# Shared expert of an MoE layer on one core: routing slots before the first chunk, and the row scatter's schedule

## The reference

```
logits = xf @ gate_w.T                      # 8 columns
probs  = softmax(logits); top 2, weights divided by their sum
shared = (silu(xf @ sw_gate) * (xf @ sw_up)) @ sw_down      # widths 256, 352, 256
shared = sigmoid(xf @ shared_gate_w.T) * shared
expert = the same gated form with w_gate[e], w_up[e], w_down[e]
x      = x + shared + sum over the token's 2 experts of weight * expert(xf)
```

## Time and profile before

| | us |
|---|---|
| median of 3 runs | 3038.25 |
| lowest and highest of them | 3037.5, 3042.67 |
| the profiled execution | 3054.86 |
| its span, first to last instruction | 3052.9 |
| stage `l1s` in it, from 980 to the first instruction of `l1e` | 980.1 to 1148.1 |

### The profile page before, as it was taken

One profiled execution on the slowest core, in us unless ns is written; L12 is line 12 of the kernel. 1 busy time (PEld: TensorE's weight loads), 2 busy tenths in 40 slices (PEclk: granted clock), 3 DMA queues, 4 the chain that ended last, 5 costly groups with the idle time before them and its releaser, 6 DMA issues. The chain is left out here.

```text
span 3052.9 us, 55088 instructions
## 1 busy us (share of the span) xinstructions
PE 2470.2 (81%) x20060; PEld 1589.0 (52%) x20060; DVE 2077.8 (68%) x5408; ACT 1273.6 (42%) x2332; POOL 1029.7 (34%) x1438
## 2 busy tenths in 40 slices
PE   1998368999617678996979887995899999969973
PEld 0444354666415347995546543444565555646662
DVE  5997746666467655665577787877766545866667
ACT  1887333333113212332347655871322222257722
POOL 3551470100254341113557478961300000025330
PEclk9998688999857889998989897996899999979996
DMA  4661555333321237775644134420200000024301
GB/s 117 178 183 52 175 210 140 96 83 107 111 79 44 76 110 264 259 259 174 222 115 100 41 104 106 92 40 3 66 22 1 1 1 1 1 53 103 74 10 61
DMA packets 320320, 300.08 MB, mean 98 GB/s; under 512 B 193244, under 2 KB 268298, under 8 KB 314037
## 3 DMA queue, kind: packets, MB, share of 16 engines
q1 hardware_dynamic: 293364, 220.28, 25.7%
q0 software_dynamic: 17904, 76.23, 7.3%
q10 hardware_dynamic: 8784, 0.04, 0.2%
HBM read 166.60 MB, written 88.34 MB: 84 GB/s over the span
## 5 line engine op out<-in xcount | busy, mean ns | idle before, releaser
L1717 ACT ACTIVATE l2e_hf<-l2e_H 128x512 f32<-128x512 f32 x208 | 124.2, 597 | 383.6 <-PE l2e_H L1658 383.6
L1871 POOL TENSOR_TENSOR all_m_rstd<-all_m_sq,all_mhalf 128x8 f32<-128x8 f32 x24 | 39.6, 1649 | 561.9 <-DVE all_m_sq L1856 527.0
L1658 PE MATMUL l0e_H<-l0e_xT,l0e_w 128*128 128x512 f16 x768 | 169.9, 383 | 27.7 <-DVE l0e_w L1736 27.7
L1771 DVE CAST l2e_hh<-l2e_hf 128x512 f16<-128x512 f32 x208 | 92.7, 446 | 123.5 <-ACT l2e_hf L1717 109.3
L805 DVE TENSOR_REDUCE l0a_mx<-l0a_S 128x2 f16<-128x512 f32 x256 | 162.3, 680 | 11.1 <-PE l0a_S L653 10.9
L1658 PE MATMUL l2e_H<-l2o_hi,l2e_w 128*128 128x512 f16 x576 | 152.5, 383 | 15.8 <-DVE l2e_w L1736 15.8
L801 DVE CUSTOM_DVE_ANT_0 l2s_masked<-l2s_S,l2s_mq 128x128 f32<-128x128 f32 (+1 forms) x512 | 149.4, 346 | 21.7 <-PE l2s_S L653 19.7
L1717 ACT ACTIVATE l0e_hf<-l0e_H 128x512 f32<-128x512 f32 x128 | 76.4, 597 | 207.4 <-PE l0e_H L1658 207.4
L1658 PE MATMUL l1e_H<-l1e_xT,l1e_w 128*128 128x256 f16 (+1 forms) x1404 | 158.7, 275 | 4.3 <-DMA l1e_w<-packed,all_second_weight_row 4.3
L761 ACT ACTIVATE l0a_pf<-l0a_ST 128x512 f32<-128x512 f32 x256 | 147.1, 610 | 23.3 <-PE l0a_ST L667 23.1
L1658 PE MATMUL l2e_H<-l2e_hh,l2e_w 128*128 128x512 f16 x640 | 155.1, 379 | 0.0
(11 more groups left out here) (687 smaller groups left out, 6999.0 us busy)
## 6 DMA issues: line engine op xcount, KB each, us to landing
l0e_wf<-in_L_ffn_w SPq DMA_DIRECT2D x16, 1024.0 KB, 7.3
rows<-l0a_zeros SPq DMA_DIRECT2D x16, 640.0 KB, 6.0
l1e_rb<-rows SPq DMA_DIRECT2D x39, 256.0 KB, 9.7
results<-l1e_y SPq DMA_DIRECT2D x39, 256.0 KB, 2.2
l0a_kv<-in_ctx SPq DMA_DIRECT2D x16, 512.0 KB, 4.2
rows<-l0a_zeros SPq DMA_DIRECT2D x16, 512.0 KB, 5.0
l0d_p_cx<-in_ctx SPq DMA_DIRECT2D x16, 512.0 KB, 5.9
results<-l0e_y SPq DMA_DIRECT2D x16, 512.0 KB, 3.0
```

Of the source, the lines that this page charges most:

```text
L1658: mm = pe.matmul(bank[0:fn, :], W[par][0:kn, at + k * wd + f0:at + k * wd + f0 + fn], X, start=(done == 0), stop=(done == k_all - 1))
L1717: nc.scalar.activation(hf[q % 4][0:fn, :], pair_of(q, lay)[0][0:fn, :], lay.func, scale=1.0 / WS).then_inc(acted, 1)
L1771: nc.vector.tensor_copy(high, v).then_inc(hi_done, 1)
L1871: self.nc.gpsimd.tensor_tensor(out=(self.rstd, self.rstd2)[which][:, g], in0=(self.sq, self.sq2)[which][:, g], in1=self.g.mhalf[:, 0:self. ...
```

## The change

It does four things, all in stage `l1s`:

- `rank` on PE and `copy_ranks` on ACT stand in front of the third chunk (q = 2), where they stood in front of the second unit (q = 3).
- DVE runs all of `assign` in one go, after `choose` and before its work on the first chunk.
- ACT makes the high halves of parts 0 to 3 first of all, ahead of the conversion of the shared weights; DVE makes the low halves of parts 0 and 1 there, and those of parts 2 and 3 right after `assign`.
- The calls are renumbered: with `BEHIND` = 0 and `EVERY` = 7, calls 0 to 3 are the four made ahead, and parts 4 to 7 fall on calls 10, 17, 24 and 31. Call 4 is the first chunk's, so part 4 goes with the first down tile of round 1, part 5 with the last, part 6 with the first down tile of round 2 and part 7 with the last.

```diff
@@ tensor queue
                 for un in plan:
-                    if router is not None and un is plan[1]:
-                        router.rank(pe)
...
                             q = un.at + f
                             before = bank_free[q]
+                            if router is not None and q == 2:
+                                router.rank(pe)
                             if before is not None:
@@ scalar queue
                 copy(0)
+                for _ in range(send.ring if send is not None else 0):
+                    send.hi_part(nc, act)
                 for k in of_expert[0]:
                     convert(k)
...
                 for un in plan:
-                    if router is not None and un is plan[1]:
-                        router.copy_ranks(act)
...
                             q = un.at + f
+                            if router is not None and q == 2:
+                                router.copy_ranks(act)
@@ vector queue
                     router.split(dve)
+                for _ in range(2 if send is not None else 0):
+                    send.lo_part(nc, dve)
                 for k in of_expert[0]:
                     convert(k)
...
                 assigning = router.assign(dve) if router is not None else iter(())
+                for _ in assigning if send is not None else ():
+                    pass
+                for _ in range(send.ring - 2 if send is not None else 0):
+                    send.lo_part(nc, dve)
@@ class Send
-    GQ, BEHIND, EVERY = 4, 11, 6
+    GQ, BEHIND, EVERY = 4, 0, 7
```

## The result

The change made the kernel slower: 3050.53 us (median of 6 runs, 3045.13 to 3051.33) against 3038.12 of the kernel before beside it (6 runs, 3036.9 to 3042.67), a ratio of 1.003 with a 95% interval of 1.002 to 1.004. The forecast was 3031. The profiled execution took 3051.33 (span 3049.6), 1 us more than its median.

The account below looks back on a forecast made before the run. Without lag, POOL's scatter bounds stage `l1s` before (1117) and PE's chain after (1106.2 + 3.7 = 1109.9), a gain of 7 us: 3038.25 - 7 = 3031. Range 3021 to 3046.

Parts of the forecast that it names:

- the first case: Stage `l1s`: no lag in timed runs, POOL bounds the kernel before; 3031 us (3028 to 3034), chance 0.45.
- the gain of 7 us: Stage `l1s` without lag: its end moves from POOL's 1117 to PE's 1110.
- the lag: Stage `l1s` during the scatter: PE halts and its finished work reaches others late; second-round down tiles lose 38.3 us.
- the second case: Stage `l1s`: lag at full size in timed runs, PE bounds both kernels; -1 to +4 us, 3037 to 3042, chance 0.32.
- I had 3.7: PE in `l1s`: late start at chunk 2 leaves it 3.7 us later after two rounds.
- the 3.6 us at the end may go: End of `l1s`: DVE's last packing began 3.6 us late; with the scatter over by then, this may vanish.
- one burst only: POOL's scatter in `l1s`, lag at full size: a burst of again 40 DMAs, keeping 38.3 us of PE's loss.
- The third case: Stage `l1s`: lag becomes longer, POOL issuing 48 DMAs in one go instead of 40; 3048 to 3052, chance 0.12.
- chunk 2 taken up 17 us later: PE in `l1s`: waits for DVE's slots and low halves, taking up chunk 2 at 1014.4, 16.6 us later.
- PE's chain alone: PE in `l1s`, kernel before without lag: its own work would end the stage at 1106.2.
- POOL's end: POOL's scatter in `l1s`, kernel before without lag: done at 1114.8, with landing and change of stage 1117.
- The ring: ACT in `l1s`: part 5's high half waits for part 1 to be sent; nothing lost, up to 1 us.

Follow-up runs that it names:

- batch D: The second batch with the lag in which both unaltered kernels ran: changed kernel 3052.18 us, kernel before 3046.65 us (29 runs).
- e10: Kernel before, with only the halves of parts 0 to 3 made ahead, all four low halves too: 0.9992 of the kernel before.
- e5: Changed kernel, unaltered, run again in a batch without the lag: 2992.61 us, 0.9947 of the kernel before.
- e16: Changed kernel with three memsets on POOL before each part but the first, in a batch with the lag: 3023.73 us, 0.9927 of the kernel before.
- e3: Changed kernel with ten memsets on POOL before each part but the first, in a batch without the lag: 1.0081 of the kernel before.
- e4: Changed kernel with one memset on POOL after each scatter DMA, in a batch without the lag: 1.0145 of the kernel before.
- e7: Changed kernel with three memsets on POOL before each part but the first, in a batch without the lag: 1.0001 of the kernel before.
- e8: Changed kernel with a very small memset (128x16) on POOL after each DMA, in a batch without the lag: 1.007 of the kernel before.
- e6: Kernel before, unaltered, run again in a batch without the lag: 0.9994 against itself.
- e15: Kernel before, with each of the four packings' low halves made twice on DVE, in a batch with the lag: 1.0021 of the kernel before.
- e12: Kernel before, with three memsets on POOL before each part but the first, in a batch without the lag: 1.004 of the kernel before, +14.2 us.

## Why the prediction was wrong

**The step that failed** is the choice of the first case, 0.45 for "no lag in the timed runs", and with it POOL as the bound of the kernel before, which alone gave the gain of 7 us. It rested on two things. One was the 16.6 us between the profiled execution of the kernel before and its median. The other was what the Trainium skill ("NOTIFIC — the notification-queue block", section "7.1 Overflow: three behaviours, one of which stalls the engine") says of the block that writes the records, that it holds its producers back rather than lose one. I took the lag for the work of a recording that timed runs don't have.

The lag was in the timed runs. With it, the profiled time of the changed kernel lies within 2 us of its median in both batches (3051.33 against 3050.53, 3050.31 against 3052.18), and breaks in the scatter bring 22 us in the median. The 16.6 us were no measure of it: that execution was already 9.5 us behind the changed kernel's at the start of the stage (980.11 against 970.63), where both kernels are still the same, and in batch D, which has the lag, 29 runs of the kernel before spread over 17 us (3036.8 to 3053.9). An unexplained difference between one execution and a median told how much the time varies, not that the lag was absent.

Whether the recording has a part in the lag is not settled by this. Every run here, not only the profiled one, comes with a span and a granted clock, so none is known to be free of records; and the traces with lag are the ones in which landing times are missing.

**What the runs showed in its place** is the second case, the lag at full size. I gave it 0.32 and -1 to +4 us, and its mechanism held: PE bound in both, lag 38.3 us in both, series of 40 DMAs in both. Its size was off: +5.3 us in the stage. After two rounds the changed kernel is 3.5 us behind in the stage (1087.17 - 970.63 against 1093.16 - 980.11); I had 3.7. Then "the 3.6 us at the end may go": the last tiles take 4.8 us less (8.1 instead of 12.9) and the two rounds of chunks 0.9 less, but 6.2 came in the third round's tiles. Parts 6 and 7 were sent in one series of 16 DMAs (24.4 us), as they had been before (1111.36 to 1134.2), and now this series ends in a round of down tiles with work left behind it. I had counted one burst only. With 1.3 us more at the change of stage the sum is 3.5 - 4.8 - 0.9 + 6.2 + 1.3 = 5.3 us, 168.0 to 173.4. The second batch's timed difference agrees (5.5). The first batch's 12.4 is 7 more, and no trace shows where; the spread of the kernel before in batch D is larger than that, in the first batch (5.8) it isn't. The third case, a longer first lag, did not come: part 5 was handed over only after it, as worked out. That its 3048 to 3052 holds the measured 3050.5 is luck.

**Right:** the first DMA 19.3 to 20.0 us earlier (20 predicted), chunk 2 taken up 17 us later (16.6), no wait at chunk 8 with the lag, 4.0 us for PE without the scatter (3.7), and a stage of 125.5 us for PE's chain alone (126.1, from 980.1 to 1106.2). The early high halves cost nothing to be seen (e10, 0.9992).

**Mis-sized, in the first case's sum.** Where there is no lag the gain was 14.3 us of stage (15.8 timed), not 7.

- *POOL's end, 13.7 us too early.* I had 137.0; it was 150.7. The DMAs from the first to the end of the last took 89.6 us, not 82.8, because packings and low halves on DVE hold POOL up: 6.8. I had named this rule and given it "about 1 us". From the end of the last DMA to the next stage it took 7.5, not 2.2: 5.3. And POOL started 1.6 later in this trace. Two of the three stood in the first trace, in stage `l0d`: its last DMA starts 8.1 us before the next stage's first load, and its slow DMAs lie beside packings.

```profile
437.14 2.42 DVE L2995 SCALAR_TENSOR_TENSOR l0d_pk_wp<-l0d_pk_wf,l0d_pk_wp 128x2176 f16<-128x2176 f32 x1
...
437.32 3.08 POOL L2622 DMA_INDIRECT rows<-l0d_parts,all_first_write  x1 [0.30 <-issue]
...
453.47 0.97 POOL L2622 DMA_INDIRECT rows<-l0d_parts,all_first_write  x1 [0.30 <-issue]
461.56 1.90 SPq L1519 DMA_TRANSPOSE l0e_xT<-rows  x1
```

- *The ring, 6.6 us instead of 0 to 1.* Without a lag POOL is behind PE, and ACT stands for part 1 to be sent before it may make part 5's high half (row of ACT in e5); chunks 6 to 11 take 22.2 us instead of the 15.5 of the later rounds. PE's chain is 136.3, of which I had 129.8.

```profile
1023.04 1.06 ACT L2605 ACTIVATE l1s_parts<-l1q_xn 128x1024 f16<-128x1024 f32 x1 [11.38 <-DMA rows<-l1s_parts,all_second_write]
```

**Open:** what the lag is. In the five traces without breaks that have it, PE first halts 17 to 19 us after the first series starts, while POOL goes on at its pitch. All of PE's halts of over half a microsecond lie in rounds of down tiles, and these begin 14 to 15.5 us after the series in all five, so how much of the delay is the series' age and how much is what PE does then isn't told apart; in e16 a round in the same place, with breaks, has no halt. Why some batches have the lag is not known, nor whether breaks of 1.3 us or series of 16 would help. No version was found that is best in both: with the lag, seven breaks (0.9927 against 1.0023 to 1.003 for the change alone); without it, the change as it stands (0.9947 against 1.0001). The breaks are the safe choice of those seen, not measurably slower than the kernel before in either.

## What to carry to other kernels

Before forecasting from a stall that nothing in the profile explains, find out whether it is there in every batch of runs; until then forecast both signs, because it decides which chain is the bound, and pulling work forward on the other chain gains nothing. Read the price of a transfer chain from a stage that does the same without company: its slow members and the time from its last issue to the next stage count as much as its pitch. And prove that a cause is present before testing its cure: the variants of e3, e4, e7 and e8 "had no lag" only because nothing in their batch had one.

## What was not expected of the hardware

- The same program on one core runs at about 3008 us in some batches and at 3038 to 3047 in others. For the changed kernel they lie 58 us apart (2992.6 and 3050.5); in the traces, 37 of them are in this one stage, 10 ahead of it and 10 behind it.
- In the batches with the lag, a round of tiles takes 38 us more (46.3 instead of 8.0), with PE idle for 28 to 32 of them, beside a series of 40 indirect DMAs that POOL issues every 1.28 us. Breaks of 2.5 to 2.7 us every 8 DMAs removed nearly all of it in the one run that tried (e16).
- A packing on DVE (2.4 us, 128x2176) holds up the indirect DMA on POOL beside it until 0.85 us after the packing's own end (e5, e6, e15 and the kernel before).
- From the start of POOL's last indirect DMA to the next stage's first work 8.2 to 8.5 us pass where POOL is the bound (e3, e4, e6 to e8, e10 to e12, e16).
